# Wide slot comparisons placed behind the addition of a superblock's sums

## The chip, the cores and the metric

The kernel runs on one core of a Trainium2 chip. The metric is the device time of one launch in microseconds; the profiled execution and three timed runs are shown below.

## The reference

Two graph layers over N = 6250 nodes with D = 64 features and E = 200000 edges sorted by target. Each layer normalises the rows, applies a relu, sends messages along edges, sums them at the target node and adds the result to x:

```
layer 0:  h = relu(layernorm(x)); g = (h @ W) * rsqrt(deg)
          x = x + h + gelu(sum over edges of g[src] * rsqrt(deg[dst]) + g * rsqrt(deg) + b)
layer 1:  h = relu(layernorm(x))
          msg(e) = relu(h[src] @ W1a + h[dst] @ W1b + edge(e) @ W1c + b1) @ W2 + b2
          agg = segment_sum(msg, dst);  x = x + mlp([agg, h])
```

## The kernel before

The second layer's messages take most of the time, and the change is there. Before the loop, `h @ W1a` is written to DRAM as `a_rows` and kept in SBUF as `atab` (three bf16 parts), and `h @ W1b + b1` is written as `b_rows`. The 200000 edges are cut into 196 superblocks of 1024 edges (T = 8 tiles of 128); four superblocks (U = 4, k = 0 to 3) make one turn of the loop, 49 turns in all. For each superblock the kernel needs the row of `a_rows` of each edge's source:

- For k = 0, 1 and 3 GpSimd gathers them from DRAM (L573, eight indirect DMAs of 128 rows each, into `rows[:, k]`), after SyncE has loaded the indices. That is 24 gathers a turn, and they follow each other on GpSimd's queue without anything between them but the wait for the indices. The descriptors of these DMAs are made on GpSimd.
- For k = 2 (KPE) the engines pick them from the table in SBUF, in two source groups of four tiles (g = 0, 1). Each group passes these stages, spread over the steps of the turn before:
  - `edges_to_slots` (L938, VectorE): four comparisons, one per tile, each 128x896 fp16, put an edge's source in the column of its slot, `to_slot`. They wait only until `to_slot` has been read.
  - `spread_slot_src` (L1443, TensorE) sums `to_slot` over the edges, ScalarE copies the result (L1150, `copy_slot_src`).
  - `picks` (L949, VectorE): 14 comparisons make one-hot matrices `pick`; `pick_rows` (L1458, TensorE) multiplies them with `atab`; ScalarE copies (L1159).
  - `slots_to_edges` (L958, VectorE): seven comparisons 128x512 make `from_slot`, which restores the order of the edges; `return_rows` (L1470, TensorE) multiplies, and `build_rows` (L966, VectorE) adds the three parts into `rows[:, 2]`.

Each superblock then goes through `transpose_edges` (L1414, PE) and its copy (L1137, ACT), `edge_and_target_terms` (L1423, PE), `add_rows` (L976, VectorE: terms plus rows), `relu` (L1142, ACT), `sum_messages` (L1432, PE, a product with the one-hot matrix that `onehots_of`, L786, made three superblocks ahead) and `add_sums` (L983, VectorE: adds the 64x64 result into `acc`, after waiting for `sum_messages` of the same superblock). Each engine has the order of its instructions written out by hand in its own `step(i, k, last)`; engines meet by semaphores alone. VectorE's step begins with a register load of the window's base (L987), then `onehots_of`, `add_rows`, the pieces of the source groups, and `add_sums` last. TensorE's step is transposes, a part of the source groups (`return_rows` at even k, `pick_rows` at odd k), the edge terms, the other part (`spread_slot_src` at even k), and `sum_messages` last. SyncE's step waits for a superblock's sum before it loads the next edges into that slot, then the next indices.

Of the kernel before, what the change touches and what calls it, by code (L numbers as in the profile page):

```python
# [20 lines left out]
def gnn_two_layers(nc: bass.Bass, x, src, dst, edge_x, l0_w, l0_b, msg_w1, msg_b1, msg_w2, msg_b2,  # L21
# [60 lines left out]
    def wide(ap, axis, n):  # L82

        shape = list(ap.shape)
        shape[axis] = n
        return ap.broadcast_to(shape)

    ctx = ExitStack()
    with ctx:
# [247 lines left out]
        def ahead(i, k, a):  # L337

            return i + (k + a) // U, (k + a) % U

        def opening(i, g):
            return isinstance(i, int) and i == 0 and g == 0
# [259 lines left out]
        def _(dve):  # L602
# [115 lines left out]
            for g in range(CH):  # L718
                k = g % 2
# [11 lines left out]
            with dve.If(passes > 1):  # L731

                with dve.Fori(0, NSB // 2) as i:
                    for k in range(2):
# [4 lines left out]
                        last = V.tensor_tensor(one_hi[:, k, :, :], digit[:, 0:HI, :],  # L739
                                               wide(dhi_b[:, cols].rearrange("p (c t) -> p c t", c=1), 1, HI), ALU.is_equal)  # L740
# [182 lines left out]
            def message_passes():  # L923
                with dve.Fori(0, passes1) as r:
# [3 lines left out]
                    def onehots_of(i, k):  # L928
                        dve.wait_ge(summed[1], r * NSB + i * U + k + 1)
                        window_onehots(i * U + k, eo[:, k, :, D:2 * D]).then_inc(onehot[1], 1)  # L930

                    def edges_to_slots(i, g):
                        n = 2 * (r * NIT + i) + g
                        if not opening(i, g):
                            dve.wait_ge(slot_src_done, 2 * n)
                        for t in range(GT):
                            e = i * T + g * GT + t
                            ins = V.tensor_scalar(to_slot[:, t, :], digit16[:, :], pe_slot[:, bass.ds(e, 1)],  # L938
                                                  pe_src[:, bass.ds(e, 1)], ALU.is_equal, ALU.mult)
                        ins.then_inc(to_slot_ready, 1)  # L940

                    def picks(i, g):
                        n = 2 * (r * NIT + i) + g
                        if not opening(i, g):
                            dve.wait_ge(picked, 4 * n)
                        for half, cols in enumerate((slice(0, SPLIT), slice(SPLIT, SLOTS_G))):
                            dve.wait_ge(slot_src_copied, 2 * n + half + 1)
                            for b in range(BLK):
                                ins = V.tensor_scalar(pick[:, b, cols], slot_src[:, cols], node_cmp[:, b:b + 1], None, ALU.is_equal)  # L949
                            ins.then_inc(pick_ready, 1)  # L950

                    def slots_to_edges(i, g):
                        n = 2 * (r * NIT + i) + g
                        dve.wait_ge(code_in[g], 16 * (r * NIT + i + 1))
                        if not opening(i, g):
                            dve.wait_ge(returned, 2 * n)
                        for b in range(BINS):
                            ins = V.tensor_scalar(from_slot[:, b, :], code_row[:, g, :], slot_cmp[:, b:b + 1], None, ALU.is_equal)  # L958
                        ins.then_inc(from_slot_ready, 1)

                    def build_rows(i, g):
                        n = 2 * (r * NIT + i) + g
                        dve.wait_ge(added, r * NSB + i * U + KPE + 1)
                        for h in range(2):
                            dve.wait_ge(returned, 2 * n + h + 1)
                            V.tensor_reduce(rows[:, KPE, g * GT + 2 * h:g * GT + 2 * h + 2, :],  # L966
                                            psum[:, 5 + h, 0:2 * NPART * D].rearrange("p (t k d) -> p t d k", k=NPART, d=D),
                                            AX, ALU.add).then_inc(rows_built, 1)

                    def add_rows(i, k):  # L970
                        if k == KPE:
                            dve.wait_ge(rows_built, 4 * (r * NIT + i + 1))
                        else:
                            dve.wait_ge(gathered[1][k], 16 * T * (i + 1))
                        dve.wait_ge(pre_done, r * NSB + i * U + k + 1)
                        V.tensor_tensor(msg[:, k % 2, :, :], psum[:, 2 + k % 2, :].rearrange("p (t d) -> p t d", d=D),  # L976
                                        rows[:, k, :, :], ALU.add).then_inc(added, 1)

                    def add_sums(i, k, b0):
                        n = r * NSB + i * U + k  # L980
                        dve.wait_ge(acc_add[1], n + 1)
                        dve.wait_ge(summed[1], n + U + 1)
                        V.tensor_tensor(acc[0:D, bass.ds(b0, W)], acc[0:D, bass.ds(b0, W)], psum[0:D, 4, 0:W],  # L983
                                        ALU.add).then_inc(acc_add[1], 1)

                    def step(i, k, last):
                        b0 = dve.value_load(base_i[0:1, bass.ds(i * U + k, 1)], min_val=0, max_val=NP - W)  # L987
                        if not last or k + 3 < U:
                            onehots_of(*ahead(i, k, 3))
                        add_rows(i, k)  # L990
                        if k == 0:
                            build_rows(i, 1)
                        if not last:
                            if k == 0:
                                picks(i + 1, 0)
                            elif k == 1:
                                slots_to_edges(i + 1, 0)
                                edges_to_slots(i + 1, 1)
                            elif k == 2:
                                build_rows(i + 1, 0)  # L1000
                                picks(i + 1, 1)
                            else:
                                slots_to_edges(i + 1, 1)
                                if not isinstance(i, int):
                                    edges_to_slots(i + 2, 0)
                        add_sums(i, k, b0)

                    dve.wait_ge(counts_reset[1], r + 1)
                    dve.sem_inc(s_turn[2], 1)
# [10 lines left out]
                    with dve.Fori(0, NIT - 2) as i:  # L1020
                        for k in range(U):
                            step(i, k, False)
                    for i in range(NIT - 2, NIT):
                        for k in range(U):
                            step(i, k, i == NIT - 1)
# [44 lines left out]
            dve.wait_ge(s_split_a, NPART)  # L1070
            dve.wait_ge(s_abd, 32)
            message_passes()

            V.memset(s1[:, :], 0.0).then_inc(s_aclr, 1)
# [481 lines left out]
```

## Time and profile before

| what | us |
|---|---|
| three timed runs | 2634.43, 2646.51, 2647.69 (median 2646.51) |
| profiled execution | 2642.74 |
| its span, first to last instruction | 2641.0 |
| TensorE matmul busy | 2303.5 (87%) |
| TensorE weight load busy | 1988.5 (75%) |
| VectorE busy | 1827.3 (69%) |
| GpSimd busy | 1829.3 (69%) |
| ScalarE busy | 1130.6 (43%) |

Busy times are unions of recorded instructions; matmuls are pipelined, so a busy TensorE isn't TensorE at its peak. A "DMA_INDIRECT" of GpSimd is the making of one gather's descriptors, not the transfer. The idle time of an engine is shown with what ended it.

### The profile page before, as it was taken

Reading aid. Unit: us, or ns where it says so; the run is one execution under the profiler, and the core shown is the slowest. Engines: PE = TensorE matmul, PEld = TensorE weight load, DVE = VectorE, ACT = ScalarE, POOL = GpSimd, SP = SyncE. Lnnn points to the kernel's source line nnn. Section 1 sums busy time; section 2 is a strip of 40 time slices with the busy share of each in tenths; the row PEclk is TensorE's granted clock in tenths of the full one; section 3 lists DMA queues with packets and bytes.
Section 4 is the critical chain, followed back from the end, with each engine's and each line's share of the span. In section 5 each row is a group of like instructions: output and inputs, shape, how many; then the busy total and the mean of one; then the engine's idle time right before and its main releaser. Section 6 shows DMA issues by size and latency. Waiting matters only on the chain.

```text
span 2641.0 us, 71244 instructions
## 1 busy us (share of the span) xinstructions
PE 2303.5 (87%) x22534; PEld 1988.5 (75%) x22535; DVE 1827.3 (69%) x5068; ACT 1130.6 (43%) x2326; POOL 1829.3 (69%) x1684
## 2 busy tenths in 40 slices
PE   2357999999994499999999999999999999999988
PEld 1246778777873378888888888888888888888874
DVE  8876777777786676666666666666666666666642
ACT  0016778878883133333333333333333333333321
POOL 2647777777770067777777777777777777777770
PEclk7569999999997699999999999999999999999986
DMA  2011111111120323333233333233223333332331
GB/s 65 1 27 27 27 28 27 28 28 28 28 28 2 71 50 64 66 65 65 63 64 65 66 65 65 65 65 65 64 63 65 66 66 66 66 65 65 64 49 24
DMA packets 349624, 134.26 MB, mean 51 GB/s; under 512 B 306107, under 2 KB 323361, under 8 KB 349473
## 3 DMA queue, kind: packets, MB, share of 16 engines
q1 hardware_dynamic: 297506, 79.11, 13.3%
q0 software_dynamic: 51968, 53.32, 10.8%
q8 instruction: 73, 1.20, 0.2%
q14 instruction: 77, 0.63, 0.1%
HBM read 124.78 MB, written 7.49 MB: 50 GB/s over the span
## 4 chain that ended last, share of the span: by engine, by line
PE 34%; POOL 32%; issue 13%; DVE 10%; DMA 6%; SPq 3%; ACT 1%; DVEq 1%; POOLq 0%; PEldq 0%; ACTq 0%
POOL rows L573 32%; PE psum L1306 8%; PE psum L1337 6%; PE psum L1458 4%; PE psum L1423 3%; DMA rows<-a_rows,idx 3%; PE psum L1432 2%; DMA idx<-src_by_tile 2%; PE psum L1470 2%; PE psum L1443 2%; PE psum L1327 2%; DVE H L949 1%; SPq L445 1%; PE psum L1414 1%; PE psum L1515 1%
## 5 line engine op out<-in xcount | busy, mean ns | idle before, releaser
L573 POOL DMA_INDIRECT rows<-a_rows,idx x1176 | 1284.1, 1092 | 496.0 <-issue 337.7
L573 POOL DMA_INDIRECT rows<-g_rows,idx x448 | 463.1, 1034 | 169.4 <-issue 135.0
L1115 ACT ACTIVATE hT<-psum 128x392 bf16<-128x392 f32 x1120 | 496.7, 502 | 139.2 <-PE psum L1337 131.8
L949 DVE TENSOR_SCALAR H<-Y,node_cmp 128x512 bf16<-128x512 f16 (+1 forms) x1372 | 383.0, 353 | 192.8 <-ACT Y L1150 192.8
L1458 PE MATMUL psum<-edge_index,H 128*128 128x192 bf16 x4802 | 430.3, 247 | 32.0 <-DVE H L949 32.0
L1306 PE MATMUL psum<-work,hT 128*128 128x192 bf16 x3430 | 447.1, 248 | 0.3 <-ACT hT L1115 0.3
L1458 PEld LDWEIGHTS psum<-edge_index,H 128*128 128x128 bf16 x4802 | 397.1, 99 | 54.9 <-issue 52.2
L1337 PE MATMUL psum<-Z,one_lo 128*128 128x392 f16 x1120 | 359.3, 342 | 28.8 <-DVE Z L827 28.6
L1423 PE MATMUL psum<-wb,eoT 128*128 128x64 f32 x3136 | 380.3, 275 | 0.0
L1306 PEld LDWEIGHTS psum<-work,hT 128*128 128x128 bf16 x3430 | 317.7, 99 | 70.6 <-issue 3.5
L1423 PEld LDWEIGHTS psum<-wb,eoT 128*128 128x128 f32 x3136 | 368.9, 193 | 0.1
L1137 ACT ACTIVATE eoT<-psum 128x512 f32<-128x512 f32 x392 | 213.0, 595 | 252.5 <-PE psum L1414 252.4
L976 DVE TENSOR_TENSOR msg<-psum,rows 128x512 f32<-128x512 f32 x196 | 133.9, 683 | 239.4 <-DMA rows<-a_rows,idx 238.8
L827 DVE TENSOR_SCALAR Z<-digit,edge_index 128x392 f16<-128x392 f16 x1120 | 290.9, 330 | 0.0
L1159 ACT ACTIVATE Y<-psum 128x384 bf16<-128x384 f32 (+1 forms) x392 | 170.9, 447 | 267.4 <-PE psum L1458 249.7
L1142 ACT ACTIVATE msg<-msg 128x512 f32<-128x512 f32 x196 | 123.3, 629 | 372.8 <-DVE msg L976 371.7
L1432 PEld LDWEIGHTS psum<-work,msg 128*64 128x64 f32 x3136 | 200.2, 139 | 67.7 <-issue 39.4
L1414 PE MATMUL psum<-ident,work 128*128 128x128 f32 x1568 | 215.8, 281 | 32.2 <-DMA work<-in_edge_attr_dram 32.2
L1470 PE MATMUL psum<-Y,Z 128*128 128x192 bf16 x2744 | 242.4, 246 | 1.5 <-DVE Z L958 1.5
L1432 PE MATMUL psum<-work,msg 128*64 128x64 f32 x3136 | 227.4, 227 | 18.0 <-ACT msg L1142 16.4
L1470 PEld LDWEIGHTS psum<-Y,Z 128*128 128x128 bf16 x2744 | 229.3, 98 | 2.9 <-DVE Z L958 1.8
L1443 PE MATMUL psum<-Y,ones 128*128 128x384 f16 (+1 forms) x784 | 169.1, 360 | 40.8 <-DVE rows L966 40.8
(237 smaller groups left out, 2140.3 us busy)
## 6 DMA issues: line engine op xcount, KB each, us to landing
work<-in_edge_attr_dram SPq DMA_DIRECT2D x390, 128.0 KB
rows<-a_rows,idx POOLq DMA_INDIRECT x1176
Z<-slot_code SPq DMA_DIRECT2D x98, 128.0 KB, 3.0
rows<-g_rows,idx POOLq DMA_INDIRECT x448
idx<-src_by_tile SPq DMA_DIRECT2D x203, 4.0 KB, 1.8
wb<-b_rows SPq DMA_DIRECT2D x196, 16.0 KB, 1.9
g_rows<-Y SPq DMA_DIRECT2D x1, 1600.0 KB, 7.1
a_rows<-Y SPq DMA_DIRECT2D x1, 1600.0 KB, 7.2
```

The source lines that it names most:

```text
L573: pool.indirect_dma_start(out=rows[:, k, t, :], out_offset=None, in_=table, in_offset=bass.IndirectOffsetOnAxis(ap=idx[:, k, t:t + 1], axis=0)
L827: V.tensor_scalar(keys[:, g * T + t, :], key_digit[:, :], key_of[:, bass.ds(tile + t, 1)], None, ALU.is_equal).then_inc(key_ready, 1)
L949: ins = V.tensor_scalar(pick[:, b, cols], slot_src[:, cols], node_cmp[:, b:b + 1], None, ALU.is_equal)
L1115: nc.scalar.activation(counts[:, j % 2, :, t * SLOTS:(t + 1) * SLOTS], psum[:, t % 4, 0:KEYS].rearrange("p (h m) -> p h m", m=SLOTS), ACT.Copy
L1306: ins = TT.matmul(psum[:, 4 + (j + 1) % 2, 0:NPART * D], counts[:, (j + 1) % 2, h, :], gtab[:, h, :, :].rearrange("p k d -> p (k d)"), sta ...
L1337: TT.matmul(psum[:, t % 4, 0:KEYS], one_lo[:, t // T, :, t % T], keys[:, t, :], start=True, stop=True).then_inc(counted, 1)
L1414: ins = TT.transpose(psum[:, h, (t % 4) * P:(t % 4 + 1) * P], eo[:, k, t, :], ident[:, :])
L1423: ins = TT.matmul(psum[:, 2 + k % 2, t * D:(t + 1) * D], eoT[:, k % 2, t, :], wb[:, k, :], start=True, stop=True)
L1432: ins = TT.matmul(psum[0:D, 4, 0:W], msg[:, k % 2, t, :], eo[:, k, t, D:2 * D], start=(t == 0), stop=(t == T - 1))
L1443: ins = TT.matmul(psum[:, 5 + half, 0:cols.stop - cols.start], ones16[:, :], to_slot[:, t, cols], start=(t == 0), stop=(t == GT - 1))
L1458: ins = TT.matmul(psum[:, PICK_BANK[u], (b % 2) * NPART * D:(b % 2 + 1) * NPART * D], pick[:, h, b * P:(b + 1) * P], atab[:, b * BLK + h, ...
L1470: ins = TT.matmul(psum[:, 5 + h, (t % 2) * NPART * D:(t % 2 + 1) * NPART * D], from_slot[:, b, t * P:(t + 1) * P], picked_rows[:, b, :], s ...
```

## The change

`edges_to_slots` leaves its place between the other comparisons and `add_sums`; it is called behind `add_sums`, in the steps k = 1 (for group 1 of the next turn) and k = 3 (for group 0 of the turn after the next). `slots_to_edges`, the comparisons that restore edge order, stays ahead of `add_sums`. No operation is added or removed, the calls before the loop stay as they are, and no other engine's program changes.

```diff
                             elif k == 1:
                                 slots_to_edges(i + 1, 0)
-                                edges_to_slots(i + 1, 1)
                             elif k == 2:
                                 build_rows(i + 1, 0)
                                 picks(i + 1, 1)
                             else:
                                 slots_to_edges(i + 1, 1)
-                                if not isinstance(i, int):
-                                    edges_to_slots(i + 2, 0)
                         add_sums(i, k, b0)
+                        if k == 1 and not last:
+                            edges_to_slots(i + 1, 1)
+                        elif k == 3 and not isinstance(i, int):
+                            edges_to_slots(i + 2, 0)
```

The loop over i runs as a hardware loop for 47 turns and is written out for the last two; k = 3 moves in the 47 alone, k = 1 in 48.

## Rows read from the trace of the kernel before

**Rows 1.** Window of the second layer's loop: PE, PEld, DVE, ACT, POOL busy, clock, DMA.
```profile
930.00:2530.00 1600.00, 1519.03 (x15754) 1369.24 (x15752) 1089.63 (x3163) 589.46 (x1147) 1243.88 (x1135) 1.00 0.30 64
```

**Rows 2.** The page's chain that ended last, share of the span by engine.
```profile
PE 34%; POOL 32%; issue 13%; DVE 10%; DMA 6%; SPq 3%; ACT 1%; DVEq 1%; POOLq 0%; PEldq 0%; ACTq 0%
```

**Rows 3.** Gathers as a group, 1000 to 2400: busy us, mean ns, idle before.
```profile
L573 POOL DMA_INDIRECT rows<-a_rows,idx x1003 | 1095.2, 1092 | 305.7 <-issue 287.1 <-DMA idx<-src_by_tile 18.6
```

**Rows 4.** Gathers over the span: shortest, median and longest ns.
```profile
L573 POOL DMA_INDIRECT rows<-a_rows,idx x1176: 940/944/4324, 917.5 to 2569.2; - x196
```

**Rows 5.** Timeline, GpSimd, step k = 3: start, us, instruction, [idle before].
```profile
1606.69 4.09 POOL L573 DMA_INDIRECT rows<-a_rows,idx  x1 [0.30 <-issue]
```

**Rows 6.** Timeline, VectorE, k = 3 into k = 0.
```profile
1606.46 0.67 DVE L976 TENSOR_TENSOR msg<-psum,rows 128x512 f32<-128x512 f32 x1
1607.06 1.91 DVE L958 TENSOR_SCALAR Z<-Z,slot_cmp 128x512 bf16<-128x512 f16 x7
1608.89 1.77 DVE L938 TENSOR_SCALAR Y<-digit,tmp_e 128x896 f16<-128x896 f16 x4
1611.49 0.22 DVE L983 TENSOR_TENSOR acc<-acc,psum 64x64 f32 x1 [0.83 <-PE psum L1432]
1612.88 0.69 DVE L786 TENSOR_TENSOR work<-iota_bw,rel 128x512 f32<-128x512 f32 x1 [1.17 <-issue]
1616.08 0.69 DVE L976 TENSOR_TENSOR msg<-psum,rows 128x512 f32<-128x512 f32 x1 [2.51 <-DMA rows<-a_rows,idx]
```

**Rows 7.** Timeline, first cycles: two more long gathers and VectorE beside them.
```profile
944.35 3.26 POOL L573 DMA_INDIRECT rows<-a_rows,idx  x1 [0.30 <-issue]
...
946.71 0.68 DVE L976 TENSOR_TENSOR msg<-psum,rows 128x512 f32<-128x512 f32 x1
...
989.72 4.32 POOL L573 DMA_INDIRECT rows<-a_rows,idx  x1 [0.30 <-issue]
...
989.72 0.67 DVE L976 TENSOR_TENSOR msg<-psum,rows 128x512 f32<-128x512 f32 x1
...
992.15 1.76 DVE L938 TENSOR_SCALAR Y<-digit,tmp_e 128x896 f16<-128x896 f16 x4
```

**Rows 8.** Waits from 1000 to 2400, waiting <- waited for: us, times, longest.
```profile
DVE msg L976 <- DMA rows<-a_rows,idx: 208.9, 84, 2.8
...
DVE H L949 <- ACT Y L1150: 155.0, 84, 2.7
...
PE psum L1443 <- DVE rows L966: 36.8, 39, 1.1
...
PE psum L1458 <- DVE H L949: 24.9, 83, 0.4
...
PE psum L1432 <- ACT msg L1142: 6.8, 24, 0.4
```

**Rows 9.** Timeline, TensorE, k = 3 into k = 0.
```profile
1610.20 1.15 PE L1432 MATMUL psum<-work,msg 128*64 128x64 f32 x16
...
1617.30 1.69 PE L1443 MATMUL psum<-Y,ones 128*128 128x512 f16 x8 [0.86 <-DVE rows L966]
```

**Rows 10.** Timeline, all engines, k = 1 into k = 2.
```profile
1626.22 0.69 DVE L976 TENSOR_TENSOR msg<-psum,rows 128x512 f32<-128x512 f32 x1 [2.71 <-DMA rows<-a_rows,idx]
1626.82 2.18 DVE L958 TENSOR_SCALAR Z<-Z,slot_cmp 128x512 bf16<-128x512 f16 x7
...
1627.63 1.15 PE L1432 MATMUL psum<-work,msg 128*64 128x64 f32 x16 [0.37 <-ACT msg L1142]
...
1628.92 1.77 DVE L938 TENSOR_SCALAR Y<-digit,tmp_e 128x896 f16<-128x896 f16 x4
...
1629.92 1.16 POOL L573 DMA_INDIRECT rows<-a_rows,idx  x1 [0.30 <-issue]
...
1632.05 1.02 DVE L966 TENSOR_REDUCE rows<-psum 128x128 f32<-128x384 f32 x2
...
1633.70 1.68 PE L1443 MATMUL psum<-Y,ones 128*128 128x512 f16 x8
```


## The prediction, made before the changed kernel was run

> **What bounds the kernel now.** I read the windows first: the loop over superblocks of the second layer takes 1600 of the 2641 us, at a granted clock of 1.00, with TensorE 95% busy and GpSimd's gathers the next [rows 1]. Then the chain of waits, where TensorE and GpSimd hold about a third each [rows 2]: neither bounds alone. The rows of GpSimd say how. In the 1400 us from 1000 to 2400 there are 1003 gathers, so a cycle of the loop (24 gathers, four superblocks) takes 24 x 1400 / 1003 = 33.5 us. A gather has a median of 944 ns and 0.305 us behind it (305.7 / 1003), and 24 x 1.249 = 30.0 us. GpSimd never waits longer than these 0.30 us, so its queue is full the whole time, and the missing 3.5 us lie in the mean of 1092 ns against the median of 944, with a largest of 4324 [rows 3, 4].
>
> Where they lie is seen in the timeline: one gather per cycle takes 4.09 us [rows 5], from 1606.69 to 1610.78. In the step of the fourth superblock (k = 3) VectorE runs seven comparisons (L958, 1607.06 to 1608.97) and the four wide ones (L938, 1608.89 to 1610.66) without a gap [rows 6]. The gather ends 0.12 us after the last of them. The start of this stage shows the same: a gather of 4.32 us ends at 994.04, 0.13 us after an L938 run that ends at 993.91; one of 3.26 us ends at 947.61, 0.22 us after an L976 at 947.39 [rows 7]. So GpSimd is held until VectorE's gapless run is over. TensorE stands behind this: of its waits 36.8 + 6.8 us hang on rows that were gathered late (L1443 waits for L966, which follows L976; L1432 waits for the relu of L976), and VectorE's L976 waited 208.9 us for gathers [rows 8]. Per cycle (1400 / 33.5 = 41.8 of them) that is 1.04 us. The other 24.9 us (L1458 for L949) is a turn TensorE to ScalarE to VectorE and back that no gather enters; it stays.
>
> **The change, part by part.** No instruction is added or removed; two groups of four L938 per cycle move behind the addition L983, in 47 cycles of the loop for k = 3 and 48 for k = 1.
>
> *k = 3.* L983 waits for TensorE's sum L1432, which ends at 1611.35 [rows 9], and so did it before (it ran at 1611.49, 0.83 us idle before it [rows 6]). L938 used that wait as cover; now it runs from about 1611.7 to 1613.5 (1.77 us). Then VectorE's next step: L786 began at 1612.88 after 1.17 us in which nothing ran (loop end and the load of a base). These run on the sequencer beside the comparisons, so L786 moves to about 1613.5 and ends at 1614.2, L976 could start at 1614.2 and L966 at 1614.9. L976 started at 1616.08, since it waits for rows [rows 6]: 1.9 us of room. TensorE's next use of the four comparisons is L1443, for which it is free at 1617.30 - 0.86 = 1616.44 [rows 9], 2.9 us after they end; L966's first half would be done at 1615.4. The move costs VectorE nothing as long as the gathered rows are later than 1614.2; without that cover it would cost at most 0.6 us.
>
> What it brings: the gapless run ends with L958, at 1608.97. The held gather ends at 1608.97 + 0.12 = 1609.09 and not at 1610.78: 1.69 us a cycle. What remains of it is 2.40 - 0.94 = 1.46 us.
>
> *The unknown price: L938 alone.* A gather can be held by the displaced run as well. Bounds: zero, if GpSimd gets in between the comparisons, as it does in the k = 1 step, where L958 and L938 also run back to back, but start from a wait for rows: there the gather that meets the end costs 1.16 - 0.94 = 0.22 us [rows 10]. Above, a gather held from its first attempt to the end of a 1.77 us run and the two instructions behind: 3.26 - 0.94 = 2.3 us [rows 7]. Runs that start right behind VectorE's earlier work hold the gather; those that start from a wait let it in: k = 1, and the L949 runs, which waited for ScalarE 84 times [rows 8] and have no long gather beside them. The displaced run starts from a wait on TensorE, so I take the near row, 0.2, and keep 0 to 2.3 for the range.
>
> *k = 1.* TensorE's sum ends at 1627.63 + 1.15 = 1628.78, before L958 ends at 1629.00 [rows 10], so L983 runs at once. Its 0.20 us now stands before L938 instead of behind it. The sequencer can prepare L938 only after that wait, for which I allow 0.2 us of gap, an estimate between nothing and the 1.17 us that L786 stood at the loop's end. L976 and L966 of k = 2 slip by this; L1443 (1633.70) came 0.63 us after L966 was done (1633.07 [rows 10]), so 0.2 is hidden, and at the upper end 0.5 us a cycle would not be. Bounds for GpSimd here: 0 to 2.3 us as above; I take 0.
>
> **The sum.** GpSimd's cycle: 33.5 - 1.69 + 0.2 = 32.0 us. TensorE's: 33.5 - 1.04 = 32.46 us. The later one decides: TensorE, 1.04 us won per cycle, 0.65 of the 1.69 unused. 47 x 1.04 = 49 us. The profiled execution took 2642.7 us (span 2641.0), so 2594; the three runs shown have a median of 2646.5, 4 us above it, and I take 2595.
>
> The Trainium skill, SBUF — State Buffer, section "Who interferes with whom", says that VectorE in a mode with two ports and GpSimd lock one pair of ports, for the whole instruction, and that whoever issues first gets it. The trace agrees on the lock (the 0.12 us after the end), not on its length: the gather was held over eleven instructions, each of 0.27 or 0.44 us (1.91 / 7, 1.77 / 4 [rows 6]). By the rule alone a hold would be below 0.5 us a gather wherever L938 stands, and the sum would be no gain.
>
> **Rivals.**
>
> *The displaced run holds a gather too (k = 3).* For it: L938 runs gapless, and a gather starts every 1.25 us, so one or two fall into it; a hold from the first attempt to the end is 1.77 less 0.6 on average, about 1.1 us. Against it: runs that start from a wait have let gathers in. GpSimd's cycle: 33.5 - 1.69 + 1.1 = 32.9, 0.6 us won, 47 x 0.6 = 28 us: 2615.
>
> *The gather's hold is not VectorE's run.* One long gather per 24 could be a thing of GpSimd's own (its loop, its descriptors). For it: one per cycle, always. Against it: the end 0.12 or 0.13 us after the run where it is followed by a wait, and the one at 944.35, before the loop's first cycle [rows 7]. Then nothing moves: 2645. By the rule of the Trainium skill cited above (SBUF — State Buffer, "Who interferes with whom") the result is the same.
>
> *Slower: the k = 1 step loses its cheap passage.* Now GpSimd slips in there at 0.22 us, since the run begins when its own rows land and so keeps step with its gathers. A gap and L983 between L958 and L938 shift L938 by some 0.3 us against the gathers; one is then held through L938 and the gapless L786 and L976 of k = 2, 2.3 us as at 944.35 [rows 7]. That decides once it costs more than the 1.69 won: 33.5 - 1.69 + 2.3 = 34.1 us, 0.6 x 47 = 28 us slower: 2673. That it can be held there at all is seen at 989.72, a k = 1 step that VectorE entered without a wait [rows 7]; against it stands that VectorE has since waited there for its rows (2.71 us [rows 10]), and then GpSimd passed.
>
> **Chances.** Forecast 0.60 (its own range 2580 to 2608: the small waits of L1458 go partly, or GpSimd needs 0.3 us more); held again at k = 3, 0.20; no gain, 0.09; slower, 0.11. A difference below 0.5% (13 us) can't be told from none here. Faster than that: forecast, nearly all of the first rival and the small outcomes between: 0.80; within it 0.09; slower 0.11. Lowest that the rows allow is all of TensorE's waits gone, (36.8 + 6.8 + 24.9) / 41.8 = 1.64 x 47 = 77 us: 2566; I start the range at 2578 and end it at 2640, short of the cases with no gain.
>
> **What would show it.** Right: the gathers of 3.9 to 4.3 us are gone and one of about 2.4 us per cycle ends 0.12 us after an L958 run; L1443's wait for L966 falls from 36.8 us per 1400 to below 8; the stretch of 24 gathers takes 32.3 to 32.6 us; GpSimd shows waits for indices longer than 0.3 us, as it is ahead. First rival: two long gathers per cycle, the second ending just behind L938. Second: one of 4.1 us still. Third: a gather of over 2 us around L938 of k = 1. The forecast is wrong if L976 of k = 0 no longer waits for rows but for VectorE's own L938, or if TensorE's cycle stays at 33.5 us with GpSimd idle.

## The result, and the profile after

The changed kernel takes 2566.37 us (median), the kernel before 2644.01 beside it: a ratio of 0.9707 (95%: 0.9684 to 0.973), 3% faster. The forecast was 2595 with a range from 2578 to 2640: the sign is right, the size is not, and the time lies 12 us below the range. The profiled executions are 2642.74 and 2561.12, 81.6 us apart against 49 forecast. One of the four runs of the changed kernel took 4267.51 us at a mean granted clock of 0.79 and is left out of this ratio; in experiments 8 and 9 the kernel before itself took 3955 to 3981 us (medians) at 0.79, so those are compared with it and with each other alone.

Where the time went is seen in the same views. First the window of the loop, with columns as in [rows 1]:

```profile
930.00:2450.00 1520.00, 1502.47 (x15715) 1363.35 (x15713) 1106.34 (x3157) 600.11 (x1144) 1161.04 (x1133) 1.00 0.32 68
```

TensorE is busy 98.8% of its loop (1502.5 of 1520), at the same granted clock of 1.00, where it was 95% [rows 1]. The loop is what became shorter: from the first transpose of its first superblock to that of its last it takes 1564.5 us, where it took 1640.5, which is 76.0 of the 81.6. The rest, 6.0 us, lies ahead of the loop, which starts at 909.6 and not at 915.6; that part of the program is the same in both, and in experiments 1 to 7 it starts between 915.7 and 921.9. The chain that ended last, which was shared between TensorE and GpSimd [rows 2], is now TensorE's:

```profile
PE 70%; DVE 11%; POOL 8%; issue 7%; ACT 2%; DVEq 1%; DMA 1%; SPq 0%; POOLq 0%; PEldq 0%; ACTq 0%
```

GpSimd's gathers from 1000 to 2400, as in [rows 3], and all of them as shortest, median and longest ns, as in [rows 4]:

```profile
L573 POOL DMA_INDIRECT rows<-a_rows,idx x1055 | 1082.0, 1026 | 321.6 <-issue 313.7 <-DMA idx<-src_by_tile 7.9
```

```profile
L573 POOL DMA_INDIRECT rows<-a_rows,idx x1176: 940/944/2632, 911.6 to 2487.2; - x196
```

24 gathers now take 24 x 1400 / 1055 = 31.8 us (33.5 before; from start to start over the same window the mean is 31.9, and 31.8 towards its end). The longest is 2.63 us instead of 4.32. The forecast step can be seen at k = 3 of one turn, GpSimd and VectorE from the timeline (lines behind the change have moved by one: L1433 is the old L1432, and so on; L573 to L983 keep their numbers):

```profile
1572.14 0.67 DVE L976 TENSOR_TENSOR msg<-psum,rows 128x512 f32<-128x512 f32 x1
...
1572.45 2.33 POOL L573 DMA_INDIRECT rows<-a_rows,idx  x1 [0.30 <-issue]
1572.74 1.91 DVE L958 TENSOR_SCALAR Z<-Z,slot_cmp 128x512 bf16<-128x512 f16 x7
...
1577.08 0.21 DVE L983 TENSOR_TENSOR acc<-acc,psum 64x64 f32 x1 [2.43 <-PE psum L1433]
...
1577.59 1.98 DVE L938 TENSOR_SCALAR Y<-digit,tmp_e 128x896 f16<-128x896 f16 x4 [0.30 <-issue]
...
1578.83 1.15 POOL L573 DMA_INDIRECT rows<-a_rows,idx  x1 [0.30 <-issue]
```

The held gather ends at 1574.78, 0.13 us behind L958 (1574.65), and the four L938, now behind L983's wait, cost the next gather 0.21 us. In other turns the comparisons hold no gather. One of them, 32 us later:

```profile
1603.46 1.55 POOL L573 DMA_INDIRECT rows<-a_rows,idx  x1 [0.30 <-issue]
1603.51 0.68 DVE L786 TENSOR_TENSOR work<-iota_bw,rel 128x512 f32<-128x512 f32 x1
1604.12 0.67 DVE L976 TENSOR_TENSOR msg<-psum,rows 128x512 f32<-128x512 f32 x1
1604.72 2.17 DVE L958 TENSOR_SCALAR Z<-Z,slot_cmp 128x512 bf16<-128x512 f16 x7
1605.31 0.95 POOL L573 DMA_INDIRECT rows<-a_rows,idx  x1 [0.30 <-issue]
```

This gather started 0.05 us ahead of L786 and ends at 1605.01, 0.82 us behind L786 (1604.19); it is through before L958 has gone far, and the next one gets in while L958 runs and pushes it instead (2.17 us against 1.91). Between 1000 and 2300 there are 18 gathers of 1.7 to 3 us, 15 at k = 3 and 3 at k = 1, and each ends 0.12 or 0.13 us behind an L958 run; 62 of 1.3 to 1.7 us; none over 3 us, where before there were 39.

The waits from 1000 to 2400, columns as in [rows 8], for the same pairs:

```profile
DVE acc L983 <- PE psum L1433: 190.3, 88, 2.6
...
PE psum L1459 <- DVE H L949: 7.0, 33, 0.3
...
DVE msg L976 <- DMA rows<-a_rows,idx: 1.5, 6, 0.3
```

VectorE's wait for gathered rows is 1.5 us instead of 208.9, TensorE's two waits on late rows (36.8 and 6.8) are gone, and its wait for the one-hot matrices is 7.0 instead of 24.9 [rows 8].

### The profile page after: what moved, and what is told of

Same layout as the page of the kernel before. It is cut to its first block, busy times and chain, and to the rows that moved or that the text cites. A ratio compares the mean times of both kernels' runs of the same rounds, so it can differ in the third digit from the quotient of the medians.

```text
span 2559.3 us, 71245 instructions
## 1 busy us (share of the span) xinstructions
PE 2284.5 (89%) x22535; PEld 1982.1 (77%) x22535; DVE 1845.3 (72%) x5068; ACT 1141.0 (45%) x2326; POOL 1744.1 (68%) x1684
## 4 chain that ended last, share of the span: by engine, by line
PE 70%; DVE 11%; POOL 8%; issue 7%; ACT 2%; DVEq 1%; DMA 1%; SPq 0%; POOLq 0%; PEldq 0%; ACTq 0%
PE psum L1459 15%; PE psum L1424 12%; PE psum L1471 8%; POOL rows L573 8%; PE psum L1307 8%; PE psum L1338 6%; PE psum L1433 5%; PE psum L1415 5%; PE psum L1444 4%; DVE H L949 3%; PE psum L1328 2%; ACT Y L1151 1%; PE psum L1516 1%; PE psum L1530 1%; PE psum L1318 1%
## 5 line engine op out<-in xcount | busy, mean ns | idle before, releaser
L573 POOL DMA_INDIRECT rows<-a_rows,idx x1176 | 1204.7, 1024 | 499.5 <-issue 349.3
L573 POOL DMA_INDIRECT rows<-g_rows,idx x448 | 457.5, 1021 | 169.0 <-issue 135.3
L949 DVE TENSOR_SCALAR H<-Y,node_cmp 128x512 bf16<-128x512 f16 (+1 forms) x1372 | 377.8, 350 | 191.9 <-ACT Y L1151 187.8
L1160 ACT ACTIVATE Y<-psum 128x384 bf16<-128x384 f32 (+1 forms) x392 | 176.5, 450 | 332.2 <-PE psum L1459 317.4
L1433 PEld LDWEIGHTS psum<-work,msg 128*64 128x64 f32 x3136 | 199.8, 139 | 55.5 <-issue 45.5
L1433 PE MATMUL psum<-work,msg 128*64 128x64 f32 x3136 | 227.0, 226 | 9.5 <-ACT msg L1143 9.5
L938 DVE TENSOR_SCALAR Y<-digit,tmp_e 128x896 f16<-128x896 f16 x392 | 190.1, 546 | 21.6 <-issue 18.4
L1415 PEld LDWEIGHTS psum<-ident,work 128*128 128x128 f32 x1568 | 169.5, 142 | 45.9 <-DMA work<-in_edge_attr_dram 31.1
```

What stands on the lines that cost most here:

```text
L573: pool.indirect_dma_start(out=rows[:, k, t, :], out_offset=None, in_=table, in_offset=bass.IndirectOffsetOnAxis(ap=idx[:, k, t:t + 1], axis=0)
L1415: ins = TT.transpose(psum[:, h, (t % 4) * P:(t % 4 + 1) * P], eo[:, k, t, :], ident[:, :])
L1433: ins = TT.matmul(psum[0:D, 4, 0:W], msg[:, k % 2, t, :], eo[:, k, t, D:2 * D], start=(t == 0), stop=(t == T - 1))
```

## The experiments

The times of experiments 1 to 7: median, and the ratio to the kernel before, run beside it on the same chip.

| kernel | us | ratio (95%) |
|---|---|---|
| 1 k = 3 moved alone | 2584.49 | 0.9759 (0.9729 to 0.9789) |
| 2 k = 1 moved alone | 2607.3 | 0.9834 (0.9769 to 0.9899) |
| 3 nothing moved, a wait ahead of L958 | 2562.51 | 0.9684 (0.9666 to 0.9701) |
| 4 nothing moved, a gap between L958 and L938 | 2574.55 | 0.9738 (0.9719 to 0.9757) |
| 5 before with half of the gathers (rows left out) | 2564.3 | 0.9696 (0.9676 to 0.9715) |
| 6 before with an addition more at k = 3 | 2636.04 | 0.9966 (0.9943 to 0.9988) |
| 7 the change and the wait of 3 | 2573.05 | 0.9743 (0.9727 to 0.976) |
| 7b the change, TensorE's edge terms first | 2559.45 | 0.9709 (0.9656 to 0.9762) |

**1 and 2: each half of the change.** The first keeps the k = 1 edit out, the second the k = 3 edit:

```diff
-                                if not isinstance(i, int):
-                                    edges_to_slots(i + 2, 0)
                         add_sums(i, k, b0)
+                        if k == 3 and not isinstance(i, int):
+                            edges_to_slots(i + 2, 0)
```

> Only the k = 3 call of edges_to_slots moves behind add_sums; k = 1 stays as before. Theory A (GpSimd was held by the gapless L958 + L938 run of k = 3, and that hold made the gathered rows late): the 3.9 to 4.3 us gathers beside k = 3 end with L958, nearly all of the gain comes: 2565 to 2585 us. Rival B (once the rows are early VectorE enters k = 1 without a wait too, and its joined eleven comparisons then hold a gather for over 3 us, so both moves are needed): gathers of 3.5 to 4.3 us appear beside k = 1 and the time stands at 2595 to 2625 us.

> Only the k = 1 call moves; k = 3 stays as before. Theory A: the long gather beside k = 3 stays (3.9 to 4.3 us, one per cycle) and the time is that of before, 2636 to 2652 us. Rival B': the order at k = 1 brings a part by itself (VectorE and GpSimd pushed against each other less): below 2630 us.

k = 3 alone brings 59 us of the 78, so k = 3 holds most of it, as forecast. Here nearly every turn shows the forecast step: 41 gathers of 2.16 to 2.62 us at k = 3 between 1000 and 2300, and none over 3 us there. TensorE's L1443 no longer waits for late rows, its L1432 still does a little (2.0 us recorded), and L976 waits for its gathers:

```profile
DVE msg L976 <- DMA rows<-a_rows,idx: 106.7, 66, 2.6
```

k = 1 alone should have brought nothing and brings 1.7% (0.9769 to 0.9899). With it 23 gathers over 3 us remain where there were 39. A k = 3 step that it lets through (GpSimd and VectorE, timeline of experiment 2):

```profile
1487.48 1.35 POOL L573 DMA_INDIRECT rows<-a_rows,idx  x1 [0.31 <-issue]
1487.93 0.67 DVE L976 TENSOR_TENSOR msg<-psum,rows 128x512 f32<-128x512 f32 x1
1488.53 2.17 DVE L958 TENSOR_SCALAR Z<-Z,slot_cmp 128x512 bf16<-128x512 f16 x7
...
1490.63 1.77 DVE L938 TENSOR_SCALAR Y<-digit,tmp_e 128x896 f16<-128x896 f16 x4
```

The same gapless L958 and L938 as before stand here, and no gather is held over them: this one started 1.05 us ahead of L958 and not 0.13 to 0.60 us as the held ones. So the hold depends on how the gather meets the run, and the edit at k = 1 has shifted that; what shifts it wasn't followed further. The two halves add to more than the whole (59 + 37 us); that each removes part of the same holds fits the counts.

**3 and 4: is it the gapless run?** Both leave the kernel before as it is and put one wait into VectorE's steps k = 1 and k = 3: experiment 3 makes L958 wait until L976 has signalled its end, experiment 4 makes L938 wait until the last L958 is done.

```diff
+                                dve.wait_ge(added, r * NSB + i * U + k + 1 + U)
                                 slots_to_edges(i + 1, 1)
```

```diff
                                 slots_to_edges(i + 1, 1)
+                                    dve.wait_ge(from_slot_ready, 2 * (r * NIT + i + 1) + 4)
                                     edges_to_slots(i + 2, 0)
```

> The order of before; VectorE's queue waits in the steps k = 1 and 3, before slots_to_edges, until its own L976 of the step is finished, so that the eleven comparisons start from a wait as they mostly did at k = 1. Theory A1 (a run that starts behind queued work keeps GpSimd out, one that starts from a wait lets it in): no gather over 2 us in the loop, time 2555 to 2580 us with eleven comparisons still gapless. Rival A2 (the length of the gapless run alone decides): gathers of 3.5 to 4.3 us stay at k = 3, time 2644 to 2655 us, the wait's own cost on top. Rival A3 (whether the gather's attempt falls before or after the first comparison's start decides): a mix, some gathers of 3.5 us and some without a hold, 2590 to 2635 us.

> The order of before; VectorE's queue waits between slots_to_edges and edges_to_slots until its own last L958 is finished, so that the run of eleven is cut by a gap of some 0.1 us and nothing stands between the two parts. Theory G (a held gather gets in at the first gap of the run): the long gathers of k = 3 end with L958 (2.1 to 2.7 us) and the time is 2560 to 2590 us. Rival (the gap must be long or a different instruction must stand in it): gathers of 3.8 to 4.4 us stay, 2640 to 2655 us.

A wait alone gives what the change gives. In experiment 3 L958 starts 0.22 us after L976, no gather between 1000 and 2400 takes 3 us and a single one over 1.7, and a gather that begins in the run takes its shortest time:

```profile
1533.02 2.15 DVE L958 TENSOR_SCALAR Z<-Z,slot_cmp 128x512 bf16<-128x512 f16 x7 [0.22 <-DVE msg L976]
1533.33 0.94 POOL L573 DMA_INDIRECT rows<-a_rows,idx  x1 [0.30 <-issue]
1534.58 0.94 POOL L573 DMA_INDIRECT rows<-a_rows,idx  x1 [0.30 <-issue]
1535.10 2.09 DVE L938 TENSOR_SCALAR Y<-digit,tmp_e 128x896 f16<-128x896 f16 x4
```

In experiment 4 L958 still follows gaplessly on queued work, the gather is held, but only to the gap:

```profile
1517.17 0.67 DVE L976 TENSOR_TENSOR msg<-psum,rows 128x512 f32<-128x512 f32 x1
1517.47 2.33 POOL L573 DMA_INDIRECT rows<-a_rows,idx  x1 [0.30 <-issue]
1517.77 1.91 DVE L958 TENSOR_SCALAR Z<-Z,slot_cmp 128x512 bf16<-128x512 f16 x7
1520.09 1.78 DVE L938 TENSOR_SCALAR Y<-digit,tmp_e 128x896 f16<-128x896 f16 x4 [0.41 <-DVE Z L958]
1520.10 1.04 POOL L573 DMA_INDIRECT rows<-a_rows,idx  x1 [0.30 <-issue]
```

It ends at 1519.80, 0.12 us behind L958, as in the changed kernel. For GpSimd, a gap of 0.4 us does what the displacement does.

**5: are the holds the cost, or what waits behind them?** The kernel before with four gathers of eight for each superblock; the rows of the other four tiles stay as they were, so its result isn't that of the reference.

```diff
-                for t in range(T):
+                for t in range(T // 2 if ring == 1 else T):
```

> The order of before, and in the second layer's loop GpSimd makes four of the eight gathers of a superblock (the rows of the other four tiles are left as they were). GpSimd is then out of the way, though it still meets VectorE. Theory A: TensorE's cycle falls to what it is in the changed kernel or below, 31.2 to 31.8 us, 2540 to 2566 us. If the changed kernel's gain came from VectorE's own order and not from late rows: about 2620 us or more.

The holds stay (42 over 3 us between 1000 and 2300), but GpSimd now idles 667.6 us for indices, and the time is that of the changed kernel. So long holds cost next to nothing while no rows are late for them; what costs is late rows. TensorE's half turn is 15.99 us by distances from start to start (16.72 before, 15.91 in the changed kernel), and what is left of the gathers' pushing shows in its wait for L949:

```profile
POOL rows L573 <- DMA idx<-src_by_tile: 667.6, 132, 11.6
...
PE psum L1458 <- DVE H L949: 21.1, 83, 0.4
```

**6: is it phase alone?** An unneeded addition of L976's shape into a spare tile, ahead of L976 at k = 3, was to start the run 0.6 us later against the gathers.

```diff
+                        if k == 3:
+                            V.tensor_tensor(spare[:, :, :], psum[:, 2 + k % 2, :].rearrange("p (t d) -> p t d", d=D),
+                                            rows[:, k, :, :], ALU.add)
```

> The order of before; in the step k = 3 the addition L976 is made twice (first into a spare tile), so that the run of eleven starts 0.6 us later against the gathers, still behind queued work and gapless. Theory P (phase: a gather is held if the run's first comparison starts 0 to 0.6 us after the gather's own start, and gets in if the run starts more than 0.6 us after it; before, it was 0.13 to 0.60 us each time): most of the gathers of over 3 us go, and the time falls to 2565 to 2610 us although VectorE does 0.6 us more in each cycle. Theory Q (a run that starts behind queued work keeps GpSimd out, whatever the phase): gathers of 4 us and more stay, 2644 to 2675 us.

The holds stay: 39 over 3 us between 1000 and 2300 (48 in the whole loop), a ratio of 0.9966. The run is longer by 0.6 us at its front, and the gathers settle against it as before:

```profile
1611.47 1.91 DVE L959 TENSOR_SCALAR Z<-Z,slot_cmp 128x512 bf16<-128x512 f16 x7
...
1611.60 4.30 POOL L574 DMA_INDIRECT rows<-a_rows,idx  x1 [0.30 <-issue]
1613.31 1.76 DVE L939 TENSOR_SCALAR Y<-digit,tmp_e 128x896 f16<-128x896 f16 x4
1615.25 0.21 DVE L987 TENSOR_TENSOR acc<-acc,psum 64x64 f32 x1 [0.18 <-PE psum L1436]
```

All but one of the long gathers now start 0 to 0.35 us behind the run's first comparison and not ahead of it. This one ends at 1615.90, 0.83 us behind the last L939 (1615.07). So do 47 of the 48 that are over 3 us (0.82 us), whether the addition L987 stands 0.16 or 0.24 us behind L939; in experiment 5, where it stands 0.80 us behind, 47 of 49 end at the same 0.82 us. It is again the end of the comparisons that lets the gather go, with more of it still to do than where 0.12 us are left. A later phase by itself frees nobody.

**7: can more be had?** The change with the wait of experiment 3; and the change with TensorE's order at k = 1 and 3 turned, the edge terms ahead of `pick_rows`.

```diff
-                        else:
-                            pick_rows(i + 1, k // 2, 0)
-                            pick_rows(i + 1, k // 2, 1)
                     (edge_and_target_terms stays here)
+                    if not last and k % 2 == 1:
+                        pick_rows(i + 1, k // 2, 0)
+                        pick_rows(i + 1, k // 2, 1)
```

> The changed kernel, and VectorE's queue waits before slots_to_edges (k = 1 and 3) for its own L976. The remaining gathers of 2.1 to 2.7 us should go (none over 1.7 us). TensorE is the bound: 0 to 6 us faster than the changed kernel, 2558 to 2568 us. If GpSimd still sets the pace there, 10 to 20 us faster.

> The changed kernel; on TensorE, in the steps k = 1 and 3, the edge and target terms come ahead of the first two picks and not behind them, so that the wait of the picks for L949 (the interval from L1415 to L1459 is 1.25 us, at least 0.93) has 1.76 us more. If TensorE alone is the bound: 0.32 us less per half cycle, 96 halves, 30 us: 2535 to 2545 us. If GpSimd (24 gathers in 31.9 us) is as much the bound as TensorE: no more than 8 us faster, 2556 to 2568 us, and the waits move to L976 and L1433.

The wait on top brings nothing: 7 us more than the changed kernel where up to 6 less were expected. The two intervals still touch (0.9727 against 0.973), so this loss isn't shown against the changed kernel; against experiment 3, the same wait without the move (0.9666 to 0.9701), it is. Gathers of 1.7 us and more fall from 18 to 2, and one that starts 0.42 us ahead of L958, where the kernel before holds it, takes its shortest time:

```profile
1343.48 0.94 POOL L573 DMA_INDIRECT rows<-a_rows,idx  x1 [0.30 <-issue]
...
1343.90 2.14 DVE L958 TENSOR_SCALAR Z<-Z,slot_cmp 128x512 bf16<-128x512 f16 x7 [0.22 <-DVE msg L976]
```

TensorE's wait for L949 rises from 7.0 to 14.3 us, and the mean distance from the transposes to the picks that wait for it from 1.25 to 1.29 us. GpSimd's 24 gathers take 31.97 us although GpSimd now waits for indices (24.3 us in all, up to 2.4 at a time), so its speed wasn't the bound any more. The turned order takes the last TensorE wait away: its profiled execution is 2538.96, with 31.2 us per 24 gathers, and GpSimd is late again (L976 waits 49.2 us for its rows, 42 times).

Its four times scatter from 2538.96 to 2576.54, unexplained, and its interval holds the changed kernel's ratio. No kernel here is shown to beat the changed one.

**8: where TensorE's remaining waits come from.** The kernel before without the second layer's gathers (L976's wait for rows goes with them, and its result isn't that of the reference).

```diff
-                for t in range(T):
+                for t in range(0 if ring == 1 else T):
```

> The order of before, and GpSimd makes no gather at all in the second layer's loop (L976 adds the rows that stand in the tile). If the picks' wait for L949 is GpSimd's pushing: L949's first seven comparisons take 1.93 us as in the best cases of the half-gathers run (2.25 before, 2.10 in the changed kernel), the interval from the transposes to the picks falls to 1.07 us (1.38 before, 1.25 after), TensorE's half cycle is 15.73 us or less, and the time 2535 to 2550 us. If it is VectorE's own order: the interval stays at 1.25 to 1.4 us and the time at 2555 to 2567 us.

The time, 2939.86 us, is far from the 2535 to 2550 expected: the part ahead of the loop, which has its own gathers, takes 1311 us here (916 in the trace of before), and the kernel before took 3981 us beside it. The loop itself can be read. It ran at a granted clock of 1.00 from 1400 to 2800, and takes 1546.6 us from its first superblock to its last, where the changed kernel takes 1564.5 and the kernel before 1640.5: of some 94 us that the gathers cost the loop, the change brings 76. TensorE has no idle time left and no wait (window from 1400 to 1600, columns as in [rows 1]):

```profile
1400.00:1600.00 200.00, 200.00 (x2100) 181.63 (x2100) 137.94 (x414) 78.33 (x152) 0.00 (x0) 1.00 0.20 44
```

The first seven L949 of a group take 1.93 us from start to end (2.25 before, 2.10 after), and TensorE's half turn is 15.73 us, as expected. So GpSimd does enter that part: its gathers push L949's comparisons, 1.67 of the seven over 400 ns before, 1.18 after, none here.

**9: orders tried against each other.** Four kernels in nine runs: the wait of 3 and the edge terms first, on the change (a) and on the kernel before (b); the edge terms first alone (c); and the change with L958 behind `add_sums` too (d).

> The changed kernel with both: VectorE waits for its own L976 before slots_to_edges, and TensorE makes the edge and target terms ahead of the first two picks. If the scatter of the terms-first kernel (2539 to 2577 us) comes from runs in which gathers are held, and the wait removes the holds: 2535 to 2548 us in all runs. If the scatter comes from pushes elsewhere (L949): it stays, median 2550 to 2570 us.

> The order of before on VectorE (edges_to_slots ahead of add_sums), with the wait for L976 before slots_to_edges and TensorE's terms first. If the order of edges_to_slots no longer matters once the gathers aren't held: the same as the kernel with the move, the wait and the terms first, within 8 us, 2535 to 2550 us. If the move has a value of its own (L983 and the relu are earlier): 10 us or more slower than it.

> The changed kernel with TensorE's terms first once more, five rounds, to see its scatter: 2539 to 2577 us in four runs before. Expected is a median of 2545 to 2565 us with single runs on both ends; if the low run was an accident, 2560 to 2575 us.

> The changed kernel, and slots_to_edges (L958) goes behind add_sums as well, ahead of edges_to_slots. No comparison stands behind queued work then, so no gather is held over 1.7 us; but from_slot is ready about 2.1 us after the sum L1433, and L1471 needs it 0.93 us after the transposes' start: TensorE waits 1.1 to 1.6 us per half cycle, 96 halves, 105 to 150 us on the changed kernel's 2566: 2670 to 2715 us. Rival: the freed GpSimd and the earlier L983 make up for it: below 2620 us.

| kernel | ratios to the kernel before, run by run |
|---|---|
| (a) | 0.991, 0.9893, 0.9937 |
| (b) | 0.9904, 0.9894 |
| (c) | 0.9879 |
| (d) | 1.0231, 1.0215, 1.026 |

(a) and (b) are the same time twice: with a gap at L958, the place of L938 shows no value of its own. (d) is 2 to 3% slower in all three, with TensorE waiting for L958 (34 us in 1400, up to 1.7 at a time), as expected; L958 can't be moved here as L938 can. All this holds for a condition in which GpSimd waits for indices up to 20 us at a time (kernel (a), 2000 to 3400):

```profile
POOL rows L573 <- DMA idx<-src_by_tile: 580.6, 78, 20.3
```

So these ratios can't be carried to the usual time, and the times that were expected of (a) to (d) are neither met nor refuted. Why the programs ran so is open. It isn't one chip: the one of experiments 4, 6 and 7 ran the kernel before at 2643.97 us and, a quarter of an hour later, at 3967.91.

## Why the prediction was right in sign and wrong in size

**The hold: right.** "The held gather ends at 1608.97 + 0.12": all 18 long gathers of the changed kernel end 0.12 or 0.13 us behind an L958 run, and experiments 3 and 4 show that it is the gapless run that holds and the gap that frees. The second rival (a thing of GpSimd's own) fell with experiment 3, in which nothing of GpSimd's program changed. The forecast that each turn has one such gather holds for k = 3 alone (experiment 1), not for the whole change: 15 of 41 turns have one at k = 3. The others meet the run as in the second timeline above.

**The price of L938 alone: right.** Forecast 0.2 us within 0 to 2.3; beside the 82 displaced runs between 1000 and 2300 the gathers take 0.14 us more than their median, 0.27 at most. The first rival fell. The gap ahead of L938, allowed with 0.2 us, is 0.15 to 0.32 us. The upper bound of 2.3 us rested on a wrong reading: the gather at 944.35 was not held by L938, which ends at that moment, but met a run of seven L958 with L786 behind it, and ended 0.82 us behind L786. The room that the move needed was there: L1444 no longer waits for L966.

**GpSimd's cycle: the number right, its make-up only in part.** Forecast 32.0 us, measured 31.9. The time over 0.944 us a gather falls from 3.56 to 1.94 us a turn, by 1.62 where 1.49 were forecast. But the held gather, expected in each turn with 1.46 us, makes up 0.61 of what is left; 0.71 come from gathers of 1.3 to 1.7 us behind L786, which the forecast had nowhere. That the two come to about the same is luck.

**TensorE's cycle: the step that failed.** "TensorE's: 33.5 - 1.04 = 32.46 us. The later one decides." Measured, as the mean distance from the start of each TensorE group to the next, over the ten groups of half a turn in the timeline (1000 to 2400, the window of the waits):

| group to next (lines of before) | before, us | after, us |
|---|---|---|
| L1423 to L1443 | 2.280 | 1.760 |
| L1443 to L1432 | 1.629 | 1.607 |
| L1414 to L1458 | 1.387 | 1.251 |
| L1458 to L1432 | 1.957 | 1.826 |
| the six others together | 9.471 | 9.469 |
| half a turn | 16.72 | 15.91 |

A turn falls from 33.45 to 31.82 us, by 1.63 and not 1.04; times 47 turns that is 77 us, and 76.0 were measured in the loop. Two terms were mis-sized:

- *The late rows were worth 1.35 us a turn, not 1.04* (2 x (0.520 + 0.022 + 0.131), the lines to L1443 and to L1432 of the table). The forecast took the recorded waits of [rows 8] for the whole loss. A wait is counted from the recorded end of the group before, and unhindered groups overlap: L1443 starts 1.76 us after L1423, whose group is recorded with 1.92 us. So each delay is 0.16 us longer there than its wait says.
- *"The other 24.9 us ... is a turn ... that no gather enters; it stays."* It was put at nothing. It fell to 7.0 us of recorded wait, and by 0.27 us a turn from start to start (2 x 0.136). Gathers enter it not as data but as a hindrance: they push L949's comparisons. Experiment 8 shows the end of that scale, 1.075 us from L1414 to L1458 with no gather, 1.251 after, 1.387 before. That fewer comparisons are pushed after the change is measured; why the gathers now meet them less often wasn't tested.

With 32.46 replaced by 31.82, the rule of the forecast (the later cycle decides) has GpSimd's 31.9 and TensorE's 31.8 next to each other, and indeed "GpSimd shows waits for indices longer than 0.3 us" did not come (one of 0.41): its queue is as full as before. What lead it has melts in the course of the loop: the last gather of superblock k = 1 is done 5.9 us ahead of its L976 at 1000 and 1.8 us at 2350, where the kernel before has a median of 1.6 us. That L1443's wait would fall below 8 us came, with 0. "The stretch of 24 gathers takes 32.3 to 32.6 us" was 31.9 for the same reason.

**k = 1: "I take 0".** Alone it brings 37 us, and without it the change loses 18 (experiments 1 and 2). Its own step has no long gather to remove; what the traces show beside it is that the k = 3 runs meet the gathers otherwise and that GpSimd has more room: in the changed kernel the last gather of superblock k = 0 starts 5.3 us ahead of its L976 (2.55 before). The slower rival, a hold at k = 1, has its place but not its price: 3 of 41 turns show a gather of 2.62 or 2.63 us there, each ended by L958's end.

The range started at 2578 although the text worked out 2566 as the lowest that the rows allow. That the result sits on that bound is luck: it took all of TensorE's waits as gone, where part of L1458's stays, and counted the late rows too low; and 6 us of the profiled difference lie ahead of the loop.

**The rule as the runs bear it out.** In the ten traces of the usual time (before, after, experiments 1 to 7) 2308 gathers of the loop took 1.03 us or more, and 2302 of them end, within 0.02 us, 0.12 or 0.82 us behind the end of a VectorE instruction. So a gather of 0.94 us seems to meet VectorE at two points, near its start (0.82 us are then left) and near its end (0.12 are left); this is read from the distances alone.

- *Near its end:* a gather that starts 0.6 to 0.1 us ahead of the first comparison of a run that VectorE enters from queued work ends 0.12 us behind the run's last comparison (48 of the 49 over 3 us in the trace of before, 0.121 to 0.127 us).
- *Near its start:* a gather that starts within such a run ends 0.82 us behind its last comparison (experiments 5 and 6). L786, which reads both inputs from SBUF, does this too, with nothing beside it: 12 of 12 gathers that start during an L786 followed by idle time in the trace of before end 0.82 us behind it. L976, which reads one of its inputs from PSUM, doesn't: of 81 gathers that start during an L976 that follows a wait, none takes over 1.0 us.
- *Let in:* a run that starts from a wait lets gathers in at the same distances. In experiments 3 and 7 (the change and the wait) all 29 that start 0.24 to 0.59 us ahead take 0.94 or 0.95 us; in 14 of them the recorded gap ahead of the run was 0.04 us. Once one is in, the next get in too, each pushing a comparison from 0.34 to 0.55 us.

The Trainium skill, SBUF — State Buffer, section "Who interferes with whom", has the lock for the length of an instruction; the traces agree that there is a lock, and measure 11 instructions under it. What inside VectorE decides it (a queue that never empties, as against one that did) fits all runs but was not measured by itself.

## What to carry to other kernels

When gathers make descriptors beside VectorE's comparisons, look for descriptors that end about 0.12 us behind a gapless VectorE run: a gap of 0.2 to 0.4 us ahead of the run or in it was worth here what the new order of the work was. A gather recorded long isn't by itself a loss. The gap pays only while someone waits for the rows. To size a loss on a pipelined engine, measure its groups from start to start and not by recorded waits, and ask of each wait of A for B what slows B.

## What the runs showed that was not expected

- A dependent wait of 0.22 us on VectorE, ahead of seven comparisons, took 81 us off the kernel (experiment 3), as much as moving eight comparisons a turn behind another wait.
- Gathers push VectorE as well as the other way round: with no gathers seven L949 take 1.93 us, with them up to 2.25.
- The change and the wait, which each bring some 80 us alone, bring 71 and no more together.
